# Two graph attention layers: the neighbour score as a column of the value matmuls, and row maxima turned in 32x32 blocks

## The chip, the cores and the metric

The kernel runs on one core of a Trainium2 chip. The metric is the device time of one execution in microseconds (us); lower is better. The engines are named as in the profile: PE (TensorE matmul), PEld (its weight load), DVE (VectorE), ACT (ScalarE), POOL (GpSimd), SP (SyncE, which issues most DMAs).

## The reference

The input is x (16 batches x 1024 nodes x 64 features, float32) and one adjacency matrix of 1024 x 1024. Four layers follow each other; each takes h = relu(layernorm(x)) and adds its result to x.

```python
def gat(h, W, a, adj):                     # layer 0 with elu, layer 3 with relu
    Wh = h @ W
    s1, s2 = Wh @ a[:64], Wh @ a[64:]
    e = leaky_relu(s1[:, :, None] + s2[:, None, :], 0.2) + mask
    return act(softmax(e, axis=2) @ Wh)
# layer 1: feat = softplus(c * x + b0); per feature softmax over neighbours of feat * wa + ba, times feat
# layer 2: four heads, h = x @ Wh.T; softmax(mask(h @ h.T)) @ h + bh; leaky_relu; one more such
#          layer over the heads' outputs with Wo; leaky_relu; layernorm with gamma, beta
```

## The kernel before, in words

**Data.** Each batch of x lies in SBUF as 128 partitions x 8 tiles (T = 8) of 64 features. One unit of work of the attention layers is one batch (layers 0 and 3) or one head of one batch (layer 2: 4 heads and one out unit a batch, 80 units). A unit has 8 steps jt, one for each 128 neighbours: a weight tile of 128 x 1024 is made in one of 8 `ring` buffers, and 32 matmuls (`weigh`, L1712) multiply it into the accumulators ACC with the values V. The column 0 of V's 65 columns carries a factor of the node, so that the sums of the weights come out beside the sums of the values.

**A unit of layers 0 and 3.** PE transposes the normalised batch (`turn_norm`, L1692), ACT writes its relu to `h_t` (L890). From `h_t` PE makes three things: the 64 value columns (`gat_columns`, L1753), the own scores f1 spread over all partitions in S (`gat_gain`, L1769), and the neighbour scores f2, 8 columns of one (`gat_peak`, L1734). Values and f2 go to the two AX banks, which a table (`AX_AT`, filled by the `place_` functions) hands out in program order. DVE copies f2 and takes its maximum over a partition (`node_max`, L1346 and L1348). PE spreads the 128 maxima over all partitions: `spread` (L1702) uses the column of maxima as weights, repeated, and the identity as the moving operand, so that each partition gets the 128 values in a row. DVE reduces them to the peak (`node_peak`, L1358), POOL makes two biases of it (L669, L671). ACT copies the values to V (L952), makes the exponentials of f2 with these biases (L958 to V's column 0, L960 to `pair_q`) and of the scores in S (L967, L970). POOL scales V by column 0 (L663). DVE makes the weight tiles, ring = max(S, pair_q) * mask (L1336). At the unit's end ACT copies ACC to `accs` (L895), DVE takes a reciprocal (L1370), and POOL divides (L639). In layer 0 POOL and ACT then make the elu (L643 above zero; L937 and L939 below) and POOL adds both parts to X (L649, L652); POOL also normalises the batches to come (L581 to L588).

**Order.** Each engine runs a program of its own, written out by hand, and waits on semaphores; an engine never passes a waiting instruction. While PE works at the sums of unit `cur`, it makes the next units' inputs at fixed steps (`gat_unit`):

```python
for jt in range(T):
    gat_sums(layer, cur, jt)
    if jt == 0 and cur + 1 < B:
        gat_nodes(layer, cur + 1)        # values, then f1
    if jt == 2 and cur + 2 < B:
        gat_peak(layer, cur + 2)         # f2
    if jt == T - 1 and cur + 2 < B:
        spread_peak(layer, cur + 2)
    if jt == T - 1 and cur + 3 < B:
        turn_norm(layer, cur + 3)
```

ACT's program of layer 0 for one `cur` is: `gat_sums` (accs), `h_relu` of cur + 2, statistics of a later batch, `gat_factors` of cur + 1 (copy of V, exponentials, scores), the elu of cur - 1, more statistics. V has three buffers, of which a unit of layers 0 and 3 uses two in turn.

**The dot layer (layer 2)** makes its weights by an exponential on ACT (L1092) and a mask on DVE (L1484); PE makes the products (L1895) and the sums (L1914). Each unit needs an upper bound of its scores: DVE sums squares (`norms`, L1513), takes their maximum over a partition (L1515), PE spreads it (L1702, the same `spread`), DVE reduces 128 columns (`bias`, L1521). The last out unit of the layer, LAST, is interleaved with the first units of layer 3 (`last_layer`); BEFORE is the unit ahead of it.

Of the kernel before, what the change touches and what calls it, by code (L numbers as in the profile page):

```python
# [11 lines left out]
P = 128  # L12
D = 64
# [17 lines left out]
def gnn_stack(nc, x, adj, w_gat0, w_gat0_t, a_gat0, w0, b0, wa, ba, wh_t, bh, wo_t, bo, gamma, beta,  # L31
# [9 lines left out]
    EARLY = 4  # L41

    with ExitStack() as ctx:
# [51 lines left out]
        V = sb("V", [P, 3, T, D + 2])  # L95
# [5 lines left out]
        f2 = sb("f2", [P, 2, T])  # L101
# [25 lines left out]
        norm2 = sb("norm2", [P, T])  # L127
# [34 lines left out]

        def chans(ap):

            return ap.unsqueeze(1).broadcast_to([P, T, D])
# [8 lines left out]

        def halves_of(ap):
            return ap.rearrange("p (h t) d -> p h t d", h=2)
# [4 lines left out]
            (w_gat[0:D, 0, 0:D], w_gat0), (w_gat[D:P, 0, 0:D], w_gat0),  # L181
            (w_gat[0:D, 1, 0:D], w_gat3), (w_gat[D:P, 1, 0:D], w_gat3),
# [49 lines left out]
        f2_copied = sem("f2_copied")  # L232
        f2_maxed = sem("f2_maxed")
# [93 lines left out]
        def gat_buf(layer, b):  # L327

            return 2 * ((b + layer // 3) % 2)
# [50 lines left out]
        def place_peak(layer, b):  # L380

            place_f2(layer, b)
            place_bias(layer, b)

# [4 lines left out]
        def place_f2(layer, b):  # L389

            for half in range(2):
                place(("GF", layer, b, half), half)

        def place_nodes(layer, b):

            for half in range(2):
                place(("GV", layer, b, half), half)

        def place_first_layer():

            place_norm(0, 0)
            place_peak(0, 0)
            place_nodes(0, 0)
            place_norm(0, 1)
            place_peak(0, 1)
# [4 lines left out]
        def place_beside(layer, cur):  # L410

            if cur + 1 < B:
                place_nodes(layer, cur + 1)
            if cur + 2 < B:
                place_peak(layer, cur + 2)
# [22 lines left out]
        for u in UNITS[:-1]:  # L438
# [11 lines left out]
            if u is BEFORE:  # L450
                place_norm(3, 0)
                place_peak(3, 0)
# [3 lines left out]
        place_nodes(3, 0)  # L456
        place_peak(3, 1)
        place_norm(3, 2)
        place_nodes(3, 1)
        place_f2(3, 2)  # L460
# [3 lines left out]
        place_nodes(3, FIRST)  # L464
        place_values(LAST)
        place_bound(LAST)
        place_peak(3, FIRST + 1)
        place_norm(3, FIRST + 2)
        for cur in range(FIRST, B):
            if cur > FIRST:  # L470
                place_beside(3, cur)
            else:
                place_nodes(3, cur + 1)
                place_peak(3, cur + 2)
                place_norm(3, cur + 3)
# [11 lines left out]
        AHEAD = 5  # L487

# [50 lines left out]
        def _(pool):  # L539
# [94 lines left out]
            def gat_divide(layer, b):  # L634
# [5 lines left out]
                if layer == 0:  # L640
# [4 lines left out]
            def gat_add(layer, b):  # L645

                if layer == 0:
# [230 lines left out]
        def _(act):  # L878
# [54 lines left out]
            def gat_below(b):  # L933

                act.wait_ge(gat_o, b + 1)
                wait(act, x_done[0], b)
                act.activation(below[:, :], o[:, :], ACT.Relu, scale=-1.0).then_inc(elu_below, 1)  # L937
                act.wait_ge(elu_below, b + 1)
                act.activation(below[:, :], below[:, :], ACT.Exp, scale=-1.0).then_inc(elu_exp, 1)  # L939

            def gat_factors(layer, b):

                gat_columns(layer, b)
                gat_gain(layer, b)

            def gat_columns(layer, b):

                n, par, buf = G0[layer] + b, b % 2, gat_buf(layer, b)
                for half in range(2):
                    k, at = AX_AT["GV", layer, b, half]  # L950
                    act.wait_ge(ax_full[k], at + 1)
                act.activation(halves_of(V[:, buf, :, 1:D + 1]), V_FULL, ACT.Copy).then_inc(gat_v_copied, 1)  # L952
                act.wait_ge(gat_v_copied, n + 1)
                for k in range(2):
                    act.sem_inc(ax_free[k], 1)
                act.wait_ge(f2_copied, n + 1)
                act.wait_ge(f2_biased, 2 * n + 2)
                act.activation(V[:, buf, :, 0], f2[:, par, :], ACT.Exp, bias=node_bias[:, par:par + 1], scale=SLOPE)\  # L958
                    .then_inc(node_made, 1)
                act.activation(pair_q[:, par, :], f2[:, par, :], ACT.Exp, bias=pair_bias[:, par:par + 1],  # L960
# [25 lines left out]
            def gat_layer(layer):  # L986
# [3 lines left out]
                for t in range(2, 5):  # L990
                    mask_copy(t)
                gat_columns(0, 0)
# [1055 lines left out]
```

## Time and profile before

| | |
|---|---|
| three runs | 1892.89, 1895.61, 1895.60 us; median 1895.60 |
| profiled execution, its own time | 1894.35 us |
| span of that execution in the trace | 1892.1 us |
| mean granted PE clock in it | 0.994 of full speed |
| busy: PE, PEld | 97%, 81% of the span |
| busy: DVE, ACT, POOL | 88%, 68%, 48% of the span |
| chain that ended last, by engine | PE 84%, POOL 8%, DVE 4%, issue 2%, ACT 1% |

The times are of whole executions; the trace is of one of them, and its span is a little shorter than that execution's time. The stages in the trace: layer 0 from about 12 to 225 us, the channel layer on PE to 405, the dot layer to 1680, layer 3 to 1890. A busy share is a mean over stages with different limits. The chain that ended last follows the work back from the end, at each step to what released it.

### The profile page before, as it was taken

To read this page: it belongs to the slowest core of one execution; us is meant where nothing else is said; L and a number is where in the kernel's file an instruction comes from. 1 tells how busy PE (TensorE), PEld (TensorE's weight loads), DVE (VectorE), ACT (ScalarE), POOL (GpSimd) and SP (SyncE) were. 2 spreads that over 40 slices of the span, in tenths; PEclk is the share of its full clock that TensorE was granted. 3 is DMA by queue.
4 is the path that set the end of the run, shared out by engine and by line. 5 is a ranking of instruction groups with operands and counts; after the bars stand their busy time and mean duration, and the time that the engine had idled before them with its cause. 6 is when DMAs were issued, how large, how long until landed. Compare 5 with 4: busy or idle time off the path is not lost.

```text
span 1892.1 us, 92007 instructions
## 1 busy us (share of the span) xinstructions
PE 1840.0 (97%) x42280; PEld 1531.0 (81%) x42280; DVE 1660.6 (88%) x1932; ACT 1285.1 (68%) x2052; POOL 907.5 (48%) x686
## 2 busy tenths in 40 slices
PE   7999899999999999999999999999999999999998
PEld 6887799987878788787888878878787878877887
DVE  6989899768898889988899888989988899888998
ACT  4998676446777777777777777777777777754332
POOL 6888999633233343424344342443334334264753
PEclk8999999999999999999999999999999999999999
DMA  7000000012111112221111211111111112201111
GB/s 192 4 4 4 3 2 3 2 25 36 37 36 36 36 36 37 34 38 31 36 34 35 38 34 36 36 36 36 36 37 36 36 35 32 42 3 26 26 32 31
DMA packets 134321, 61.02 MB, mean 32 GB/s; under 512 B 122416, under 2 KB 122672, under 8 KB 133936
## 3 DMA queue, kind: packets, MB, share of 16 engines
q1 hardware_dynamic: 131712, 54.55, 14.3%
q8 instruction: 332, 5.44, 1.2%
q10 hardware_dynamic: 2224, 0.59, 0.1%
q14 instruction: 53, 0.43, 0.1%
HBM read 8.98 MB, written 4.19 MB: 7 GB/s over the span
## 4 chain that ended last, share of the span: by engine, by line
PE 84%; POOL 8%; DVE 4%; issue 2%; ACT 1%; DMA 0%; ACTq 0%; POOLq 0%; DVEq 0%
PE ACC L1914 30%; PE S L1895 29%; PE S L1872 8%; PE ACC L1712 7%; PE AX L1957 3%; PE AX L1930 2%; DVE ring L1336 1%; PE AX L1702 1%; PE AX L1692 1%; POOL above L643 1%; PE S L1769 1%; POOL o L639 1%; DVE ring L1484 1%; PE AX L1753 1%; POOL X L649 1%
## 5 line engine op out<-in xcount | busy, mean ns | idle before, releaser
L1484 DVE TENSOR_TENSOR ring<-ring,mask_self_t 128x1024 f32<-128x1024 f32 x640 | 878.0, 1385 | 68.8 <-ACT ring L1092 61.1
L1092 ACT ACTIVATE ring<-S,dot_bias 128x1024 f32<-128x1024 f32 x640 | 711.5, 1113 | 274.3 <-PE S L1895 235.7
L1914 PEld LDWEIGHTS ACC<-V,ring 128*64 128x64 f32 x20480 | 706.7, 138 | 109.8 <-issue 13.2
L1914 PE MATMUL ACC<-V,ring 128*64 128x65 f32 x20480 | 708.0, 222 | 0.0
L1895 PE MATMUL S<-FA 128*64 128x512 f16 x5120 | 665.5, 380 | 1.1 <-ACT ring L1092 0.9
L1895 PEld LDWEIGHTS S<-FA 128*64 128x64 f16 x5120 | 268.6, 110 | 141.8 <-issue 10.9
L1336 DVE SCALAR_TENSOR_TENSOR ring<-S,pair_q,mask_t 128x1024 f32<-128x1024 f32 x256 | 313.9, 1273 | 16.5 <-issue 4.3
L1712 PEld LDWEIGHTS ACC<-V,ring 128*64 128x64 f32 x8192 | 253.3, 139 | 56.2 <-DVE ring L1336 34.7
L1712 PE MATMUL ACC<-V,ring 128*64 128x65 f32 x8192 | 270.4, 225 | 20.3 <-DVE ring L1336 11.5
L819 POOL TENSOR_TENSOR EV_both<-score,recip 128x512 f32<-128x512 f32 x64 | 96.8, 1512 | 263.9 <-DVE score L1494 263.8
L1872 PE MATMUL S<-parts,mask_t 128*128 128x128 bf16 x3072 | 173.8, 220 | 4.7 <-DVE o L1461 3.5
L1872 PEld LDWEIGHTS S<-parts,mask_t 128*128 128x128 bf16 x3072 | 173.2, 98 | 5.3 <-issue 5.3
L812 POOL TENSOR_TENSOR V<-v_plain,bh_bc 128x512 f32<-128x512 f32 x64 | 99.8, 1559 | 124.3 <-ACT v_plain L1119 124.3
L1502 DVE TENSOR_TENSOR HL<-v_plain,HL 128x512 f16<-128x512 f32 x80 | 77.0, 962 | 76.7 <-ACT HL L1124 76.7
L895 ACT ACTIVATE accs<-ACC 128x520 f32<-128x520 f32 x32 | 19.1, 597 | 90.7 <-PE ACC L1712 90.7
L819 POOL TENSOR_TENSOR relu_z<-score,recip 128x512 f32<-128x512 f32 x16 | 16.7, 1042 | 124.6 <-DVE score L1494 124.6
L557 POOL TENSOR_TENSOR st_x<-X,st_mean 128x512 f32<-128x512 f32 x20 | 33.5, 1676 | 75.0 <-DVE st_mean L1303 75.0
L600 POOL TENSOR_TENSOR ln_xc<-X,ln_mean 128x512 f32<-128x512 f32 x16 | 22.5, 1409 | 95.7 <-DVE ln_mean L1319 95.7
L802 POOL TENSOR_TENSOR sp_log<-relu_z,on_mean 128x512 f32<-128x512 f32 x16 | 30.5, 1906 | 74.5 <-DVE on_mean L1531 74.5
L663 POOL TENSOR_TENSOR V<-V 128x512 f32<-128x512 f32 x32 | 33.3, 1041 | 59.9 <-ACT V L958 59.8
L1459 DVE RECIPROCAL ch_rden<-S 128x512 f32<-128x512 f32 x15 | 50.3, 3351 | 10.6 <-PE S L1872 7.8
L1513 DVE TENSOR_REDUCE norm<-sq 128x8 f32<-128x512 f32 x80 | 54.0, 675 | 0.0
(149 smaller groups left out, 2076.6 us busy)
## 6 DMA issues: line engine op xcount, KB each, us to landing
FA<-FA SPq DMA_DIRECT2D x160, 128.0 KB, 2.3
X<-in_x SPq DMA_DIRECT2D x16, 256.0 KB, 4.8
ring<-in_adj SPq DMA_DIRECT2D x8, 512.0 KB, 8.1
out_x<-X SPq DMA_DIRECT2D x16, 256.0 KB, 2.6
FA<-HL SPq DMA_TRANSPOSE x80, 3.1
wh<-in_wh_t ACTq DMA_DIRECT2D x2, 64.0 KB, 6.5
bh_bc<-in_bh ACTq DMA_DIRECT2D x1, 128.0 KB, 9.9
w_gat<-in_w_gat ACTq DMA_DIRECT2D x4, 16.0 KB, 3.9
```

Source lines behind the costliest of these rows:

```text
L812: pool.tensor_tensor(V[:, u["n"] % 3, :, 1:D + 1], plain_of(u), chans(bias), ALU.add)\
L819: pool.tensor_tensor(dst, tiles(leaky[:, :]), cols(recip[:, :]), ALU.mult).then_inc(z_epi, 1)
L1092: act.activation(ring[:, jt, :], S[jt % 2][:, :], ACT.Exp, bias=dot_bias[:, n % 2:n % 2 + 1])\
L1336: dve.scalar_tensor_tensor(out=ring[:, jt, :], in0=S[par][:, :], scalar=pair_q[:, par, jt:jt + 1], in1=mask_t[:, jt, :], op0=ALU.max, op1= ...
L1484: dve.tensor_tensor(ring[:, jt, :], ring[:, jt, :], mask_self_t[:, jt, :], ALU.mult)\
L1502: dve.tensor_tensor(HL[:, par, :, D:2 * D], plain_of(u), HL[:, par, :, 0:D], ALU.subtract)\
L1513: dve.tensor_reduce(norm2[:, :], tiles(sq[:, :]), AX_X, ALU.add).then_inc(bound_dve, 1)
L1712: last = pe.matmul(acc_of(t)[rows, :], ring[:, jt, t * P + c * CUT:t * P + (c + 1) * CUT], values, start=(jt == 0 and t % 4 == 0), stop=(j ...
L1872: last = pe.matmul(S[par][:, t * P:(t + 1) * P], mask_t[:, j, t * P:(t + 1) * P], parts[:, k % 3, part, j, :], start=(j == 0 and part == 0 ...
L1895: last = pe.matmul(S[jt % 2][rows, cut], FA[:, buf, 0, jt * P + c * CUT:jt * P + (c + 1) * CUT], FA[:, buf, i, cut], start=(i == 0), stop= ...
L1914: last = pe.matmul(acc_of(t)[rows, :], ring[:, jt, t * P + c * CUT:t * P + (c + 1) * CUT], V[:, n % 3, jt, 1:D + 2], start=(jt == 0 and t ...
L1957: last = pe.matmul(AX[half][c * CUT:(c + 1) * CUT, t * width:(t + 1) * width], rows, w, start=(i == 0), stop=(i == chunks[-1]), skip_group ...
```

## The change

The f2 column moves into the value matmuls: `w_gat` now holds it as column 0 ahead of the 64 value columns, and `gat_columns` makes 65 columns for each tile. `gat_peak` on PE and its places in AX_AT are gone. The value matmuls of unit cur + 2 stand after the third tile of unit cur, where f2's stood. ACT copies all 65 columns to V one unit sooner; for that V has four buffers, and a unit uses three in turn. In layer 0 this copy (of cur + 2) stands ahead of the exponentials of cur + 1, in layer 3 behind them. DVE reads f2 from V's column 0.

The maxima of f2 and of the norms are reduced further before the spread: DVE transposes 32x32 blocks, so that the values of 32 partitions come to lie in one row, and reduces over 32; `spread` then moves 32 columns in place of 128, with a strided identity, and DVE's reductions behind it read 32.

For the last two batches of layer 0 (`ELU_SWITCH`) the elu is made in another way: POOL takes min(o, 0), ACT its exponential, DVE max(exp - 1, o), and POOL adds once. The start of layer 3 is put in an order that fits the earlier values.

On ACT, in the middle of layer 0, a unit stood so before (accs is the copy of the sums, h_t the relu, st_x the statistics, V<-AX the copy of the values, V<-f2 and pair_q the exponentials):

```order
L895 ACTIVATE accs<-ACC 128x520 [waits gat_o,pv_done]
L890 ACTIVATE h_t<-AX 128x512 [waits ax_full1]
L915 ACTIVATE st_x,st_shift<-X 128x64 [waits h_ready,late_squared,x_in12]
L915 ACTIVATE st_x,st_shift<-X 128x64 x7
L952 ACTIVATE V<-AX 128x8x64 [waits ax_full1,ax_full0]
L958 ACTIVATE V<-f2,node_bias 128x8 [waits gat_v_copied,f2_biased,f2_copied]
L960 ACTIVATE pair_q<-f2,pair_bias 128x8
L967 ACTIVATE S1<-S1,f2_peak 128x1024 [waits f1_full]
L970 ACTIVATE S1<-S1,pair_lift 128x1024 [waits gain_clamped]
```

and now:

```order
L895 ACTIVATE accs<-ACC 128x520 [waits gat_o,pv_done]
L890 ACTIVATE h_t<-AX 128x512 [waits ax_full1]
L915 ACTIVATE st_x,st_shift<-X 128x64 [waits h_ready,late_squared,x_in12]
L915 ACTIVATE st_x,st_shift<-X 128x64 x7
L949 ACTIVATE V<-AX 128x8x65 [waits ax_full1,ax_full0]
L964 ACTIVATE V<-f2,node_bias 128x8 [waits gat_v_copied,f2_biased,f2_copied]
L966 ACTIVATE pair_q<-f2,pair_bias 128x8
L973 ACTIVATE S1<-S1,f2_peak 128x1024 [waits f1_full]
L976 ACTIVATE S1<-S1,pair_lift 128x1024 [waits gain_clamped]
```

The rows stand in the same places, but the copy V<-AX is now that of unit cur + 2, where it was that of cur + 1; the exponentials behind it are still those of cur + 1.

On PE, the beginning of a unit of layer 0 before (ACC<-V,ring are the sums, AX<-w_gat,h_t 64x64 the values, 64x1 f2, S1<-h_t,w_gat the scores f1):

```order
L1712 MATMUL ACC<-V,ring 64x65 [waits weight_done,acc_copied,v_scaled]
L1712 MATMUL ACC<-V,ring 64x65 x15
L1753 MATMUL AX<-w_gat,h_t 64x64 [waits ax_free1,ax_free0]
L1753 MATMUL AX<-w_gat,h_t 64x64 x15
L1769 MATMUL S1<-h_t,w_gat 64x512 [waits weight_done]
L1769 MATMUL S1<-h_t,w_gat 64x512 x3
L1712 MATMUL ACC<-V,ring 64x65 [waits weight_done]
L1712 MATMUL ACC<-V,ring 64x65 x15
L1712 MATMUL ACC<-V,ring 64x65 [waits weight_done]
L1712 MATMUL ACC<-V,ring 64x65 x15
L1734 MATMUL AX<-w_gat,h_t 64x1 [waits ax_free1,ax_free0,h_ready]
```

and now:

```order
L1744 MATMUL ACC<-V,ring 64x65 [waits weight_done,acc_copied,v_scaled]
L1744 MATMUL ACC<-V,ring 64x65 x15
L1782 MATMUL S1<-h_t,w_gat 64x512 [waits weight_done]
L1782 MATMUL S1<-h_t,w_gat 64x512 x3
L1744 MATMUL ACC<-V,ring 64x65 [waits weight_done]
L1744 MATMUL ACC<-V,ring 64x65 x15
L1744 MATMUL ACC<-V,ring 64x65 [waits weight_done]
L1744 MATMUL ACC<-V,ring 64x65 x15
L1766 MATMUL AX<-w_gat,h_t 64x65 [waits ax_free1,ax_free0,h_ready]
L1766 MATMUL AX<-w_gat,h_t 64x65 x15
L1744 MATMUL ACC<-V,ring 64x65 [waits weight_done]
```

The value matmuls moved from behind the first tile to behind the third, took f2's place, and belong to a unit further ahead.

On DVE, in the dot layer, the bound of a unit before (ring<-ring,mask_self_t is the masking of a weight tile):

```order
L1513 TENSOR_REDUCE norm2<-sq 128x8 [waits sq_made]
L1515 TENSOR_REDUCE norm2_max<-norm2 128x1 [waits bound_dve]
L1484 TENSOR_TENSOR ring<-ring,mask_self_t 128x1024 [waits exp_done] x3
L1521 TENSOR_REDUCE norm2_all<-AX 128x1 [waits ax_full0]
L1523 TENSOR_SCALAR dot_bias<-norm2_all 128x1 [waits ax_free0]
```

and now:

```order
L1543 TENSOR_REDUCE norm2<-sq 128x8 [waits sq_made]
L1545 STREAM_TRANSPOSE norm2_turned<-norm2 128x32 [waits bound_dve]
L1547 TENSOR_REDUCE norm2_max<-norm2_turned 128x1 [waits bound_dve]
L1514 TENSOR_TENSOR ring<-ring,mask_self_t 128x1024 [waits exp_done] x3
L1553 TENSOR_REDUCE norm2_all<-AX 128x1 [waits ax_full0]
L1555 TENSOR_SCALAR dot_bias<-norm2_all 128x1 [waits ax_free0]
```

One transposition stands between the two reductions; the third reduction reads 32 columns of AX.

The diff, cut to its core:

```diff
-        V = sb("V", [P, 3, T, D + 2])
+        V = sb("V", [P, 4, T, D + 2])
...
+        def turned_cols(ap):
+            return ap.rearrange("p (g r) -> p g r", r=SQ)[:, :, 0:T]
...
-            return 2 * ((b + layer // 3) % 2)
+            return (0, 1, 2)[b % 3] if layer == 0 else (2, 3, 0)[b % 3]
...
# POOL
+                if layer == 0 and b >= ELU_SWITCH:
+                    pool.tensor_scalar(below[:, :], o[:, :], 0.0, None, ALU.min).then_inc(elu_below, 1)
...
# ACT
             def gat_columns(layer, b):
...
-                act.activation(halves_of(V[:, buf, :, 1:D + 1]), V_FULL, ACT.Copy).then_inc(gat_v_copied, 1)
+                act.activation(halves_of(V[:, buf, :, 0:D + 1]), V_GAT, ACT.Copy).then_inc(gat_v_copied, 1)
...
+            def gat_factors(layer, b):
+                gat_exponents(layer, b)
+                gat_gain(layer, b)
...
                     if late_stats(layer, cur) is not None:
                         late_shifts(late_stats(layer, cur))
+                    if cur + 2 < B:
+                        gat_columns(layer, cur + 2)
                     if cur + 1 < B:
                         gat_factors(layer, cur + 1)
...
                     if cur + 1 < B:
                         gat_factors(3, cur + 1)
+                    if cur + 2 < B:
+                        gat_columns(3, cur + 2)
...
# DVE
             def node_max(layer, b):
...
+                dve.wait_ge(gat_v_copied, n + 1)
                 wait(dve, pair_made, n - 1)
+                dve.tensor_copy(f2[:, par, 0:T], V[:, gat_buf(layer, b), :, 0]).then_inc(f2_copied, 1)
+                dve.wait_ge(f2_copied, n + 1)
+                dve.transpose(f2_turned[:, :], f2[:, par, :]).then_inc(f2_across, 1)
+                dve.wait_ge(f2_across, n + 1)
+                dve.tensor_reduce(f2_max[:, :], f2_turned[:, :], AX_X, ALU.max).then_inc(f2_maxed, 1)
...
+            def gat_elu(b):
+                dve.wait_ge(elu_exp, b + 1)
+                dve.scalar_tensor_tensor(out=o[:, :], in0=below[:, :], scalar=-1.0, in1=o[:, :],
+                                         op0=ALU.add, op1=ALU.max).then_inc(elu_made, 1)
...
             def norms(u):
...
-                dve.tensor_reduce(norm2_max[:, :], norm2[:, :], AX_X, ALU.max).then_inc(bound_dve, 1)
+                dve.transpose(norm2_turned[:, :], norm2[:, :]).then_inc(bound_dve, 1)
+                dve.wait_ge(bound_dve, n + 2)
+                dve.tensor_reduce(norm2_max[:, :], norm2_turned[:, :], AX_X, ALU.max).then_inc(bound_dve, 1)
...
# PE
             def spread(k, column):
                 for c in range(2):
-                    last = pe.matmul(AX[k][c * CUT:(c + 1) * CUT, 0:P], column.broadcast_to([P, CUT]), ident[:, :],
-                                     start=True, stop=True, skip_group_check=True)
+                    last = pe.matmul(AX[k][c * CUT:(c + 1) * CUT, 0:T * P // SQ], column.broadcast_to([P, CUT]),
+                                     turned_cols(ident[:, :]), start=True, stop=True, skip_group_check=True)
...
                     gat_sums(layer, cur, jt)
                     if jt == 0 and cur + 1 < B:
-                        gat_nodes(layer, cur + 1)
+                        gat_gain(layer, cur + 1)
                     if jt == 2 and cur + 2 < B:
-                        gat_peak(layer, cur + 2)
+                        gat_columns(layer, cur + 2)
```

## Rows read from the trace of the kernel before

**Rows 1.** Windows: busy us (x instructions) of each engine, granted clock, DMA share, GB/s.
```profile
85.90:155.00 69.10, 65.66 (x2020) 57.10 (x2016) 61.95 (x73) 63.05 (x265) 60.93 (x67) 1.00 0.02 4
...
440.00:1660.00 1220.00, 1218.20 (x26716) 977.01 (x26714) 1086.01 (x1289) 896.43 (x1128) 447.48 (x265) 1.00 0.18 36
```

**Rows 2.** Timeline, a unit of layer 0: start, duration, engine, line, operation, [idle before].
```profile
114.14 1.15 PE L1712 MATMUL ACC<-V,ring 128*64 128x65 f32 x32 [0.16 <-issue]
...
115.22 0.69 PE L1753 MATMUL AX<-w_gat,h_t 64*64 64x64 f32 x32
...
115.74 1.04 PE L1769 MATMUL S<-h_t,w_gat 64*64 64x512 f32 x8
...
116.72 0.58 ACT L952 ACTIVATE V<-AX 128x512 f32<-128x512 f32 x1
...
117.99 0.31 ACT L958 ACTIVATE V<-f,node_bias 128x8 f32<-128x8 f32 x1 [0.69 <-POOL pair_bias L671]
...
118.44 1.04 POOL L663 TENSOR_TENSOR V<-V 128x512 f32<-128x512 f32 x1 [0.55 <-ACT V L958]
...
118.72 0.64 PE L1734 MATMUL AX<-w_gat,h_t 64*64 64x1 f32 x32
...
119.30 4.89 PE L1712 MATMUL ACC<-V,ring 128*64 128x65 f32 x160
...
123.72 1.04 POOL L588 TENSOR_TENSOR ln_y<-ln_xc,st_rstd 128x512 f32<-128x512 f32 x1
...
125.63 1.15 PE L1712 MATMUL ACC<-V,ring 128*64 128x65 f32 x32 [0.16 <-issue]
```

**Rows 3.** Timeline, a unit of layer 3, the values and what follows on ACT.
```profile
1801.93 0.69 PE L1753 MATMUL AX<-w_gat,h_t 64*64 64x64 f32 x32
...
1802.78 0.60 ACT L952 ACTIVATE V<-AX 128x512 f32<-128x512 f32 x1 [1.24 <-PE AX L1753]
...
1803.62 0.31 ACT L958 ACTIVATE V<-f,node_bias 128x8 f32<-128x8 f32 x1 [0.24 <-ACT V L952]
```

**Rows 4.** Timelines of PE and POOL, first to last units of layer 0.
```profile
45.79 0.69 PE L1753 MATMUL AX<-w_gat,h_t 64*64 64x64 f32 x32
...
161.46 0.69 PE L1753 MATMUL AX<-w_gat,h_t 64*64 64x64 f32 x32
...
164.22 1.04 POOL L663 TENSOR_TENSOR V<-V 128x512 f32<-128x512 f32 x1 [1.52 <-ACT V L958]
...
186.80 0.69 PE L1753 MATMUL AX<-w_gat,h_t 64*64 64x64 f32 x32
...
190.02 1.04 POOL L663 TENSOR_TENSOR V<-V 128x512 f32<-128x512 f32 x1 [2.37 <-ACT V L958]
```

**Rows 5.** Window and PE timelines at the end of layer 0.
```profile
217.70:221.10 3.40, 2.67 (x50) 2.67 (x52) 3.40 (x4) 1.32 (x3) 3.32 (x3) 0.50 0.02 5
...
218.43 4.23 PE L1712 MATMUL ACC<-V,ring 128*64 128x65 f32 x96 [2.80 <-DVE ring L1336]
...
250.61 5.58 PE L1872 MATMUL S<-parts,mask_t 128*128 128x128 bf16 x68 [3.50 <-DVE o L1461]
```

**Rows 6.** Chain that ended last (one piece), then timelines, dot layer.
```profile
1671.21 0.22 PE AX L1702 x4
...
479.94 0.44 PE L1702 MATMUL AX<-ident,norm_max 128*64 128x128 f32 x4
...
1656.59 0.16 DVE L1515 TENSOR_REDUCE norm_max<-norm 128x1 f32<-128x8 f32 x1
...
1656.81 0.44 PE L1702 MATMUL AX<-ident,norm_max 128*64 128x128 f32 x4
```

**Rows 7.** Timelines, start of layer 3 (DVE, PE) and a steady unit (DVE).
```profile
1683.74 1.28 DVE L1336 SCALAR_TENSOR_TENSOR ring<-S,pair_q,mask_t 128x1024 f32<-128x1024 f32 x1 [4.29 <-issue]
...
1701.92 2.08 PE L1957 MATMUL AX<-wo,z_t 128*64 128x64 f32 x64 [1.05 <-ACTq L955]
...
1811.26 0.29 DVE L1358 TENSOR_REDUCE f_peak<-AX 128x1 f32<-128x128 f32 x1 [0.28 <-PE AX L1702]
```

More of the change, by code:

```diff
@@ L463, in gnn_stack @@
         place_norm(3, 3)
-        place_nodes(3, FIRST)
         place_values(LAST)
         place_bound(LAST)
[L467 to L475, printed above, removed]
+        for cur in range(FIRST - 1, B):
+            place_beside(3, cur)
         def stats_before(layer):
@@ L645, in gat_add @@
             def gat_add(layer, b):
-                if layer == 0:
+                if layer == 0 and b >= ELU_SWITCH:
+                    pool.wait_ge(elu_made, b + 1)
+                    pool.tensor_tensor(x_of(b), x_of(b), tiles(o[:, :]), ALU.add).then_inc(x_done[layer], 1)
+                elif layer == 0:
                     pool.wait_ge(elu_above, b + 1)
@@ L933, in gat_below @@
             def gat_below(b):
-                act.wait_ge(gat_o, b + 1)
-                wait(act, x_done[0], b)
-                act.activation(below[:, :], o[:, :], ACT.Relu, scale=-1.0).then_inc(elu_below, 1)
+                if b < ELU_SWITCH:
+                    act.wait_ge(gat_o, b + 1)
+                    wait(act, x_done[0], b)
+                    act.activation(below[:, :], o[:, :], ACT.Relu, scale=-1.0).then_inc(elu_below, 1)
                 act.wait_ge(elu_below, b + 1)
[L939 to L944, printed above, removed]
+                act.activation(below[:, :], below[:, :], ACT.Exp, scale=-1.0 if b < ELU_SWITCH else 1.0)\
+                    .then_inc(elu_exp, 1)
             def gat_columns(layer, b):
-                n, par, buf = G0[layer] + b, b % 2, gat_buf(layer, b)
+                n, buf = G0[layer] + b, gat_buf(layer, b)
                 for half in range(2):
@@ L989, in gat_layer @@
                 h_relu(0, 0)
-                for t in range(2, 5):
-                    mask_copy(t)
+                mask_copy(2)
                 gat_columns(0, 0)
+                mask_copy(3)
+                mask_copy(4)
+                gat_exponents(0, 0)
                 mask_copy(5)
@@ L1416, in gat_layer @@
                                 channel_part(k, k % 2, (1, 3, 6, 7).index(jt))
+                        if jt == 7 and cur > ELU_SWITCH:
+                            gat_elu(cur - 1)
             def channel_step(k, par):
@@ L1723, in gat_sums, with gat_columns @@
                 weigh(tile_of(layer, b, jt), jt, V[:, buf, jt, 0:D + 1])
[L1725 removed]
+            def gat_columns(layer, b):
                 w = layer // 3
                 pe.wait_ge(h_ready, H0[layer] + b + 1)
[L1729 to L1747 removed]
                 for half in range(2):
```

146 lines of the change are left out of this document (66 added, 80 removed).

## The prediction

> **What bounds the kernel now.** I looked first at the busy table by stage [rows 1]. In the long dot layer (440 to 1660 us) PE is busy 1218.20 of 1220.00 us, so there only PE time counts, or a wait that PE gains. In the middle of layer 0 (85.9 to 155.0) no engine is full: PE 65.66, ACT 63.05, POOL 60.93 and DVE 61.95 of 69.10. Such a stage is bounded by a loop that passes through several engines, and a busy share says nothing of what an edit costs. So I laid one unit of it out as a timeline [rows 2]. A unit starts with PE's first weight tile, at s = 114.14; the next starts at 125.63, so the period is 11.49 us. Within it ACT waits 0.69 us for POOL's pair_bias, makes the exponentials at 117.99, and POOL in turn waits 0.55 us for them before it scales V at 118.44. POOL then works without a long pause until ln_y (123.72, 1.04 us long), PE transposes that, and the next unit begins. The loop is POOL, ACT, POOL; from the exponentials to the next first tile it takes 125.63 - 117.99 = 7.64 us. The copy of V sits just ahead of them on ACT at 116.72, with no wait before it, because PE made the values early, at 115.22.
>
> **Layer 0, the loop.** The change makes the values one unit sooner, but after the third tile of the unit instead of the first, where the f2 matmuls stood. On ACT the copy of these values is put ahead of the exponentials of the next unit. ACT runs in order, so the exponentials, which needed only POOL's bias, now wait for PE's third tile.
>
> On PE, f2 started at s + 4.58 (118.72 - 114.14). The values no longer lie ahead of it, which moves everything up by 0.52 (115.22 to 115.74), so the new value matmuls start at s + 4.06.
>
> From their start to ACT's copy, and from that to the exponentials: in layer 3 [rows 3] ACT already waits for the values. There the matmuls start at 1801.93, the copy at 1802.78 (0.85 later), the exponentials at 1803.62 (0.84 later). So in layer 0 the copy would start at s + 4.91, the exponentials at s + 5.75; before it was 117.99 - 114.14 = 3.85.
>
> The rest of the loop is unchanged, 7.64. The period becomes 5.75 + 7.64 = 13.39 us, **+1.9 us a unit**.
>
> The first unit of this form has its values at 45.79 and the eleventh at 161.46 [rows 4]: ten periods, 115.67 us, of which 134.0 would be made, +18.3. Three more units follow, longer ones, where POOL's scaling already came later: 164.22 - 161.46 = 2.76 and 190.02 - 186.80 = 3.22 after the values' start. With the new order it is 4.06 - 1.08 (first tile to values, 115.22 - 114.14) + 0.85 + 0.84 + 0.45 (117.99 to 118.44) = 5.12 by the same mark, so +2.4 and +1.9; at their mean three units give +6.4. Together **+24.7**. The lower end is one in which the three long units absorb it (+18).
>
> PE's removed f2 matmuls (32 in 0.58 us, 118.72 to 119.30) are worth nothing here, and neither does the 65th column of the values cost anything: the loop runs past PE with room. No DMA is added or moved, the two more small copies of w_gat's columns come once, at the start, for which I take 0, with 1 us either way. The work of DVE (a copy, a transpose, a reduction per unit) lies beside the loop too. node_max now waits for ACT's copy, which would end at s + 5.5, and the sixth weight tile stands behind it on DVE; PE wants that tile at about s + 4.64 + 3 x 0.98 = s + 7.6, so there is little room, but what is late there comes out of PE's pause at the unit's end. If that cover were gone it would cost 0.2 us a unit, one small DVE operation.
>
> **Layer 0, the clock.** PE's own work of a unit does not grow, so the idle time does. The last sums would end at s + 4.06 + 0.58 (values) + 4.75 (160 matmuls in 4.89 less a pipeline tail, from 119.30) = s + 9.4, and ln_y is ready for PE at s + 5.75 + 6.77 (117.99 to 123.72 + 1.04) = s + 12.5: about 3.1 us idle in each unit. In the trace an idle time of 2.80 us ahead of 218.43 is followed by a granted clock of 0.50 (1.2 instead of 2.4 GHz) from 217.7 to 221.1 [rows 5], and 96 sums then took 4.23 us, where 96 at the rate of 119.30 take 2.93. So one fall costs 1.3 us at most and about 1.2 in the loop, where a piece of it is in the shadow of the idle time. It lies between the first tile and the values, that is on the loop. I take 8 of 13 units, **+10**; bounds 0 (none falls) and +16 (all).
>
> **Layer 0, the end.** For the last two batches one POOL pass, and the ACT pass ahead of the exponential, are dropped. PE waits 3.50 us ahead of 250.61 for what follows from it [rows 5]; that bounds the gain. I take **-2.3**, two thirds, ends 0 and -3.5.
>
> **Dot layer.** The transposition of the bound costs DVE one more operation in each of the 80 units, and the spread on PE reads 32 instead of 128 columns. A spread costs 0.22 us in the chain (1671.21) [rows 6]. Its new price lies between 32 matmuls of one column in 0.58 (118.72 to 119.30), that is 0.07 for four, and 65 columns, 160 in 4.89, that is 0.12 for four [rows 2]. I take 0.09, which saves 0.13. But norm_max begins at 1656.59 and lasts 0.16, and PE's spread begins at 1656.81 [rows 6]: at that place PE hangs on it, and it is so in 30 of the 80 units, from the one with its spread at 479.94 to this one, by my count of the gap; in one the slack is 0.23 and in 49 at least 0.39 us. The trace of before has no such transposition; the nearest rows are small DVE operations, 0.16 (norm_max) and 0.29 (f_peak over 128 columns, [rows 7]). I take 0.18, with two handovers 0.24. In 30 units 0.24 - 0.13 = 0.11 is lost (+3.3), in 50 units 0.13 is won (-6.5): **-3.2**. If the transposition is hidden everywhere, -10.4; if the spread saves nothing, 30 x 0.24 = +7.2.
>
> A rule of the Trainium skill speaks against this part. The page "TensorE: Matmul & The Clock Gate", section "LDWEIGHTS (loading the stationary operand)", says a weight load takes its columns divided by 1.2, in ns; the spread still loads 64 columns, four times, so by my estimate 0.21 us would remain and nothing be saved. The rows here speak against that: 160 sums, each with a load of 64 columns, took 30.6 ns apiece [rows 2].
>
> **Layer 3.** Here the new copy stands behind the exponentials, so nothing waits for it. A steady unit gains where PE and DVE hand over to each other, at the spread and the peak: DVE's reduction waits 0.28 for PE at 1811.26 [rows 7]. With 32 columns that is 0.13 for the spread and 0.10 for the reduction, against 0.03 for one more step in the chain of node_max: -0.2 a unit, eleven units, -2.2. The start of the layer is put in another order. DVE was idle 4.29 us ahead of 1683.74, and PE waited 1.05 ahead of 1701.92 for ACT's copy, which is now behind it; I take -3.1 of these 5.3 together (0 to -5). **-5.3**, from -2 to -7.
>
> **The sum.** 24.7 + 10 - 2.3 - 3.2 - 5.3 = +23.9. The profiled execution took 1894.35 us, so 1918.3; the median of the three runs, 1895.60, lies 1.25 above it, so on that scale 1919.5. I say **1919.0**.
>
> **The rivals.**
>
> **First**, the clock holds. The loop lengthens, but the spread of f2_max, now free to run in the pause, splits the idle time. Then 1894.35 + 13.9 = 1908.3. For it: the 3.1 is only 0.3 over the shortest idle time with a fall. 22%.
>
> **Second**, the wait does not bind, and the kernel is **faster**. The mechanism: PE reaches its third tile early relative to ACT. It decides at copy's start: ACT comes free for it at s + 2.58 (116.72), and if it could start by s + 3.01 (3.85 less 0.84), the exponentials would stay where they are. That needs PE 1.9 us further ahead of ACT than in [rows 2]. Then only the other terms are left: -2.3 - 3.2 - 5.3, 1883.6. Against it: PE's first tile itself hangs on ln_y, at the end of the same loop, so it cannot run ahead. 8%.
>
> **Third**, the spread is bound by its weight loads and saves nothing. +7.2 instead of -3.2 in the dot layer, and with the forecast otherwise, 1929. It is also what the rule on weight loads would make of it. 8%.
>
> **Fourth**, the change does little: the loop lengthens by only a part, because something in it (POOL's other work, ACT's statistics) is moved into the new wait, and the gains cancel it, 1891 to 1900. 5%.
>
> The forecast itself, loop and clock, has 57%; within it the number of falls spreads it from 1909 to 1926.
>
> **How the numbers follow.** About 0.2%, 3.8 us, is what a measurement of this kernel can tell from no change. Faster: the second rival alone, 0.08. Same: the last, 0.05. Slower: the rest, 0.87. The range 1901 to 1932 takes in the forecast with all its bounds, the held clock and the load-bound spread, and leaves out the faster case and part of the last.
>
> **What would show it.** In the changed profile a layer 0 unit should last 13.4 to 14.6 us; ACT's copy of V should wait over 2 us for PE's value matmuls, POOL's scaling over 2 us for ACT's exponentials; PE's granted clock in the middle of layer 0 should lie below 1.00 with 3 us idle ahead of the transposes of ln_y. In the dot layer the spread should take about 0.1 us, with DVE's norm_max 0.2 us later. Layer 3 should be some 5 us shorter. I am wrong if the period of layer 0 stays at 11.5, or if DVE's transposition takes far more than 0.3 us.

## The result, and the profile after

The change took 1947.84 us (median of 4 runs, 1943.47 to 1950.80) against 1895.61 of before: a ratio of 1.0276, 95% interval 1.0262 to 1.0290. It is slower, as forecast, but by 52 us and not by 24; 1919.0 (1901 to 1932) was too low. The profiled execution took 1943.47 us, span 1941.4, 49.3 more than before; the median lies 4.4 us above it, where before it was 1.25.

To see where the time went I cut both traces at the same places: the first score matmul (S<-h_t,w_gat) of the third, the 13th and the 16th unit of layer 0, the first spread of the dot layer, a late one, and the end. The times between them, us:

| stretch | before | change | difference | forecast |
|---|---|---|---|---|
| start to the third unit | 46.31 | 48.05 | +1.7 | 0 |
| ten units of layer 0 | 115.66 | 147.56 | +31.9 | +18.3, and falls |
| the three long units | 37.15 | 49.10 | +12.0 | +6.4, and falls |
| end of layer 0 and channel layer | 200.40 | 196.34 | -4.1 | -2.3 |
| dot layer, first to late spread | 1257.28 | 1259.28 | +2.0 | -3.2 |
| end of the dot layer and layer 3 | 235.32 | 241.10 | +5.8 | -5.3 |

The falls of the clock were forecast at +10 for the second and third line together. The first line differs by up to 5 us between runs of these kernels, so nothing is read from it.

The windows of the change (busy us of PE, PEld, DVE, ACT, POOL, then granted clock, DMA share, GB/s):

```profile
105.00:145.00 40.00, 31.73 (x912) 27.36 (x912) 31.29 (x39) 31.58 (x131) 30.33 (x33) 1.00 0.01 3
145.20:152.40 7.20, 6.16 (x70) 4.10 (x72) 4.92 (x5) 4.34 (x26) 5.16 (x7) 0.53 0.01 2
...
85.90:155.00 69.10, 55.01 (x1468) 46.61 (x1466) 51.27 (x62) 51.83 (x218) 50.02 (x55) 0.93 0.01 3
440.00:1660.00 1220.00, 1209.56 (x26565) 965.10 (x26564) 1095.91 (x1360) 888.82 (x1119) 447.31 (x263) 1.00 0.19 36
```

The third and fourth answer to [rows 1]. In the same 69.1 us of layer 0 every engine now does less, none is nearer to full. PE has pauses at the full clock (31.73 of 40.00 busy) and at half of it (6.16 of 7.20): each engine waits for another. One unit at the full clock, from the timeline (start, duration, engine, line, operation, [idle before]), answers to [rows 2]:

```profile
120.14 1.15 PE L1744 MATMUL ACC<-V,ring 128*64 128x65 f32 x32 [0.15 <-issue]
...
124.26 0.69 PE L1766 MATMUL AX<-w_gat,h_t 64*64 64x65 f32 x32
...
125.11 0.60 ACT L949 ACTIVATE V<-AX 128x520 f32<-128x520 f32 x1 [2.29 <-PE AX L1766]
...
125.95 0.31 ACT L964 ACTIVATE V<-f,node_bias 128x8 f32<-128x8 f32 x1 [0.24 <-DVE f L1367]
...
126.41 1.04 POOL L663 TENSOR_TENSOR V<-V 128x512 f32<-128x512 f32 x1 [2.51 <-ACT V L964]
...
131.69 1.04 POOL L581 TENSOR_TENSOR ln_y<-ln_xc,st_rstd 128x512 f32<-128x512 f32 x1
...
132.78 0.66 PE L1724 MATMUL AX<-ident,ln_y 128*128 128x128 f32 x4 [2.72 <-POOL ln_y L581]
...
133.59 1.15 PE L1744 MATMUL ACC<-V,ring 128*64 128x65 f32 x32 [0.15 <-issue]
```

This is the forecast loop nearly to the digit: the value matmuls start at s + 4.12 (forecast 4.06), ACT's copy waits 2.29 us for them and starts at s + 4.97 (4.91), the exponentials at s + 5.81 (5.75), POOL waits 2.51 for them, and the unit lasts 133.59 - 120.14 = 13.45 us (13.39). PE's pause ahead of ln_y is 2.72 (3.1), and 2.68 to 2.73 in all twelve such units; the clock falls behind nine of these pauses and not behind those of 105.87, 119.33 and 132.78.

What the forecast did not have stands in layer 3, in the timeline of a steady unit of the change:

```profile
1875.84 1.27 POOL L655 TENSOR_TENSOR X<-X,o 128x512 f32<-128x512 f32 x1
1875.94 1.20 DVE L1367 COPY f<-V 128x8 f32<-128x8 f32 x1
...
1877.17 0.21 DVE L1369 STREAM_TRANSPOSE f_turned<-f 128x32 f32<-128x32 f32 x1
1877.42 0.18 DVE L1371 TENSOR_REDUCE f_max<-f_turned 128x1 f32<-128x32 f32 x1
...
1878.85 2.35 PE L1744 MATMUL ACC<-V,ring 128*64 128x65 f32 x64 [0.91 <-DVE ring L1359]
```

DVE's copy of 128x8 values lasts 1.20 us and ends with POOL's addition to X; the next weight tiles stand behind it, and PE waits 0.91 for them. Before the change the copy read PSUM (AX) and was short, also beside a TENSOR_TENSOR of POOL:

```profile
1806.08 1.04 POOL L581 TENSOR_TENSOR ln_xc<-X,st_mean 128x512 f32<-128x512 f32 x1
...
1806.84 0.15 DVE L1346 COPY f<-AX 128x8 f32<-128x8 f32 x1
...
1812.83 0.69 PE L1753 MATMUL AX<-w_gat,h_t 64*64 64x64 f32 x32
```

A unit takes 11.70 us, where before it was 10.90 (1801.93 to 1812.83 for the value matmuls).

### The profile page after: what moved, and what is told of

It is laid out like the page before. It is cut to its first block, busy times and chain, and to the rows that moved or that the text cites. A ratio compares the mean times of both kernels' runs of the same rounds, so it can differ in the third digit from the quotient of the medians.

```text
span 1941.4 us, 89972 instructions
## 1 busy us (share of the span) xinstructions
PE 1841.1 (95%) x41256; PEld 1522.0 (78%) x41256; DVE 1694.0 (87%) x2050; ACT 1284.9 (66%) x2050; POOL 905.7 (47%) x684
## 4 chain that ended last, share of the span: by engine, by line
PE 61%; DVE 21%; POOL 6%; ACT 5%; issue 5%; DMA 0%; ACTq 0%; POOLq 0%; DVEq 0%
PE S L1906 20%; PE ACC L1925 19%; DVE ring L1514 10%; PE S L1883 8%; PE ACC L1744 6%; DVE ring L1359 4%; PE AX L1968 3%; ACT ring L1103 3%; PE AX L1941 2%; DVE norm L1543 1%; DVE HL L1532 1%; PE S L1782 1%; PE AX L1724 1%; POOL above L640 1%; POOL o L632 1%
## 5 line engine op out<-in xcount | busy, mean ns | idle before, releaser
L1514 DVE TENSOR_TENSOR ring<-ring,mask_self_t 128x1024 f32<-128x1024 f32 x640 | 864.4, 1370 | 59.8 <-ACT ring L1103 54.6
L1925 PEld LDWEIGHTS ACC<-V,ring 128*64 128x64 f32 x20480 | 707.2, 138 | 109.7 <-issue 13.2
L1925 PE MATMUL ACC<-V,ring 128*64 128x65 f32 x20480 | 708.3, 222 | 0.1
L1906 PEld LDWEIGHTS S<-FA 128*64 128x64 f16 x5120 | 263.2, 110 | 141.4 <-issue 10.9
L1744 PEld LDWEIGHTS ACC<-V,ring 128*64 128x64 f32 x8192 | 266.0, 144 | 79.8 <-DVE ring L1359 43.9
L1744 PE MATMUL ACC<-V,ring 128*64 128x65 f32 x8192 | 286.1, 230 | 33.9 <-DVE ring L1359 22.2
L812 POOL TENSOR_TENSOR V<-v_plain,bh_bc 128x512 f32<-128x512 f32 x64 | 113.6, 1774 | 119.0 <-ACT v_plain L1130 119.0
L1532 DVE TENSOR_TENSOR HL<-v_plain,HL 128x512 f16<-128x512 f32 x80 | 91.5, 1143 | 72.9 <-ACT HL L1135 72.9
L1724 PE MATMUL AX<-ident,ln_y 128*128 128x128 f32 x192 | 35.4, 313 | 33.6 <-POOL ln_y L581 32.7
L949 ACT ACTIVATE V<-AX 128x520 f32<-128x520 f32 x32 | 19.3, 604 | 61.8 <-PE AX L1766 61.8
```

The source lines that it names most:

```text
L812: pool.tensor_tensor(V[:, u["n"] % 3, :, 1:D + 1], plain_of(u), chans(bias), ALU.add)\
L1514: dve.tensor_tensor(ring[:, jt, :], ring[:, jt, :], mask_self_t[:, jt, :], ALU.mult)\
L1532: dve.tensor_tensor(HL[:, par, :, D:2 * D], plain_of(u), HL[:, par, :, 0:D], ALU.subtract)\
L1724: last = pe.transpose(AX[k][:, q * P:(q + 1) * P], ln_y[:, q * P:(q + 1) * P], ident[:, :])
L1744: last = pe.matmul(acc_of(t)[rows, :], ring[:, jt, t * P + c * CUT:t * P + (c + 1) * CUT], values, start=(jt == 0 and t % 4 == 0), stop=(j ...
L1906: last = pe.matmul(S[jt % 2][rows, cut], FA[:, buf, 0, jt * P + c * CUT:jt * P + (c + 1) * CUT], FA[:, buf, i, cut], start=(i == 0), stop= ...
```

## The experiments

Each is compared with before on its own chip. "Ten units" and so on are the stretches of the table.

**1. The exponentials ahead of the copy.** ACT's order in layer 0:

```diff
+                    if cur + 1 < B:
+                        gat_exponents(layer, cur + 1)
                     if cur + 2 < B:
                         gat_columns(layer, cur + 2)
                     if cur + 1 < B:
-                        gat_factors(layer, cur + 1)
+                        gat_gain(layer, cur + 1)
```

> In layer 0 ACT makes the two exponentials of unit cur + 1 ahead of the copy of unit cur + 2, instead of behind it; all else is the change. Theory A (the exponentials queue behind a copy that waits for PE's third tile): a unit of layer 0 returns from 13.46 us to about 11.5, PE's pauses of 2.73 us and the falls of its clock with them go, layer 0 shortens by some 40 to 45 us, total 1901 to 1909. Rival B (the longer chain on DVE, copy, transposition and reduction behind ACT's copy, bounds the unit by itself): the period stays above 12.5 and the total above 1920.

Measured: 1926.39 us, 1.0170 (1.0155 to 1.0185). Ten units took 137.36 us, so still 13.7 each: rival B's numbers, and my theory wrong in the form that I gave it. But DVE is not the reason. The timeline, in a unit with its first part at half the clock:

```profile
114.70 0.59 ACT L895 ACTIVATE accs<-ACC 128x520 f32<-128x520 f32 x1
...
115.38 2.00 PE L1746 MATMUL ACC<-V,ring 128*64 128x65 f32 x32 [2.48 <-issue]
...
117.87 0.29 ACT L964 ACTIVATE V<-f,node_bias 128x8 f32<-128x8 f32 x1
...
121.70 0.60 ACT L949 ACTIVATE V<-AX 128x520 f32<-128x520 f32 x1 [3.35 <-PE AX L1768]
```

The exponentials come early again (117.87, s + 2.5), and POOL is served. But ACT now waits 3.35 us at the copy with all the rest of its unit behind it: the scores, the elu, the statistics, and last the copy of the sums to accs, without which PE may not begin the next unit. That copy ends at 115.29, and PE, idle for 2.48 us, starts at 115.38. So there were two loops through the same wait; freeing the one leaves the other.

**2. PE kept busy in its pause.** Forty matmuls of the identity, whose result nothing reads, are added ahead of the transposes of ln_y in 13 units:

```diff
                     if jt == T - 1 and cur + 3 < B:
+                        if layer == 0:
+                            k = take_bank(AX_AT["T", layer, cur + 3])
+                            for _ in range(40):
+                                pe.matmul(AX[k][:, 0:P], ident_bf[:, :], ident_bf[:, :], start=True, stop=True,
+                                          skip_group_check=True)
                         turn_norm(layer, cur + 3)
```

> The change, with 40 matmuls of the identity (no result used, into a free bank of AX) in PE's pause at the end of the first 13 units of layer 0, ahead of the transposes of ln_y. Theory A (the lengthened loop alone costs about 26 us in layer 0, and the rest of its 45.5 us are falls of the clock, each dearer than the 1.2 us I took): no granted clock of 0.50 between 60 and 240 us, the period 13.46 in each of the units 1 to 10, total about 18 to 20 us shorter than the change, 1927 to 1930. Rival B (a fall costs the 1.2 us of the prediction, ten falls 12 us, and the rest is a longer wait in the loop): total 1934 to 1938. Rival C (the clock falls whether PE is busy in the pause or not): no change, 1944 to 1950.

Measured: 1929.07 us, 1.0185 (1.0170 to 1.0200), 18.8 below the change: theory A. The windows:

```profile
62.00:210.00 148.00, 140.87 (x3771) 124.06 (x3772) 119.58 (x152) 112.66 (x452) 107.08 (x116) 1.00 0.01 4
228.00:235.20 7.20, 6.47 (x98) 4.64 (x96) 6.64 (x9) 5.50 (x11) 6.74 (x8) 0.53 0.01 2
```

The clock stays at 1.00 from 62 to 210 us. Two falls follow, at 214.6 and 228.3 us: they lie in the last units, after the added matmuls, but still inside the 240 us that theory A had named. Ten units take 135.24 us: 134.0 was forecast for the loop. Against the change's 147.56 that is 12.3 us for the seven falls in this stretch, 1.8 each.

**3. f2 taken by a reduction.** One instruction:

```diff
-                dve.tensor_copy(f2[:, par, 0:T], V[:, gat_buf(layer, b), :, 0]).then_inc(f2_copied, 1)
+                dve.tensor_reduce(f2[:, par, 0:T], V[:, gat_buf(layer, b), :, 0:1], AX_X, ALU.max).then_inc(f2_copied, 1)
```

> The change, with DVE's copy of f2 out of V (128x8, 1.20 us in a steady unit of layer 3, 0.17 in layer 0) written as a reduction over one element, which does the same work. Theory A (the copy, SBUF to SBUF, waits for POOL's addition to X, which runs just then and ends with it; a reduction doesn't): the operation takes about 0.16 us in layer 3, its units return from 11.70 to 10.7 to 10.9 us, 9 to 11 us less in total, 1936 to 1940. Rival B (the copy is slow for its strided source or waits for ACT's write of V): as slow as before, 1944 to 1950. Rival C (the operation gets short, but another wait in layer 3 takes its place): period above 11.3, under 4 us less.

Measured: 1934.96 us (1930.83 to 1939.15), 1.0214 (1.0194 to 1.0234). The runs scatter with the falls in layer 0, so the reading rests on the stretch of layer 3: 230.31 us against 241.10, and a steady unit 10.73. About 0.6 of these 10.8 us is not the copy but a fall of the clock at 1749.7 us in the change's profile, which this one hasn't (the same fall makes layer 3 of experiment 8 below 0.55 longer than that of 7). The timeline:

```profile
1876.80 1.28 POOL L655 TENSOR_TENSOR X<-X,o 128x512 f32<-128x512 f32 x1
1876.98 0.15 DVE L1367 TENSOR_REDUCE f<-V 128x8 f32<-128x8 f32 x1
```

The same values from the same place beside the same addition, in 0.15 us: theory A.

**4. The dot layer's bound as before.** No transposition in `norms`, 128 columns in `spread` and `bias` for the dot layer alone.

> The change, with the bound of the dot layer made as before (no transposition, the spread of 128 columns, the reduction of 128); the attention layers keep theirs. Theory A (DVE is full in two units of each batch, the transposition adds there what it lasts, +0.45 and +0.15 us, and three units win 0.13 each: +0.2 a batch): dot layer 2 to 4 us shorter, total 1943 to 1946. Rival B (the shorter spread wins more than the transposition costs, and the 2 us lie in the phase of POOL's work): dot layer 3 to 10 us longer, total 1951 or more.

Measured: 1943.42 us (1940.06 to 1949.26), 1.0253 (1.0236 to 1.0270). The total tells nothing, since the runs scatter by 9 us with the falls in layer 0 (ten units 152.99 in the profiled execution). The dot layer took 1259.07 us, where the change took 1259.28: 0.2 shorter, by itself neither theory. From the eleventh unit on, the turned bound does lose 0.2 us a batch (+0.45, +0.15 and three times -0.13), as theory A has it; but in the first batch the plain bound falls 2.5 us behind the turned one, once. The traces show why. PE's pause ahead of ln_y in this batch is 1.79 us with the plain bound and 0.91 with the turned one, which gives 0.85; and behind the longer pause the clock fell to 0.50 in this run and in experiment 6, the other one with the plain bound, but not in the kernel before (first two lines before the change, the others experiment 6):

```profile
447.79 0.66 PE L1692 MATMUL AX<-ident,ln_y 128*128 128x128 f32 x4 [1.79 <-POOL ln_y L615]
449.00:452.40 3.40, 3.40 (x82) 2.73 (x78) 1.45 (x3) 2.43 (x3) 0.00 (x0) 1.00 0.02 5
...
440.89 0.66 PE L1722 MATMUL AX<-ident,ln_y 128*128 128x128 f32 x4 [1.81 <-POOL ln_y L608]
442.10:445.50 3.40, 3.40 (x44) 2.55 (x40) 0.94 (x1) 1.60 (x2) 0.00 (x0) 0.50 0.02 5
```

From the fourth spread to the fifth it took 18.56 us in both runs with the fall and 16.93 before the change: the fall costs 1.6 us. Without it the plain bound would be 1.8 us shorter here than the change's, just under theory A's 2 to 4. The kernel before, with the plain bound and no fall, is 2.0 shorter.

**5. The copy late.** ACT's copy behind exponentials and scores in layer 0, node_max two tiles later:

```diff
-                    if cur + 2 < B:
-                        gat_columns(layer, cur + 2)
                     if cur + 1 < B:
                         gat_factors(layer, cur + 1)
+                    if cur + 2 < B:
+                        gat_columns(layer, cur + 2)
...
-                        if jt == 5 and cur + 2 < B:
+                        if jt == 7 and cur + 2 < B:
                             node_max(layer, cur + 2)
```

> The change, with ACT's copy of unit cur + 2 behind the exponentials and the scores of cur + 1 in layer 0 (as layer 3 has it), and DVE's node_max behind the eighth weight tile instead of the sixth. Theory A, as the run with the exponentials ahead of the copy left it (not the exponentials but everything that ACT still has to do in the unit stands behind the wait for PE's third tile, down to the copy of the sums, for which PE's next unit waits; a copy that finds its values ready costs nothing): a unit of layer 0 takes 11.4 to 11.7 us, no falls of the clock in units 1 to 10, total 1899 to 1908. Rival B (the third tile is too late for DVE's f2 chain wherever the copy stands): 12.5 us or more a unit, total above 1918.

Measured: 1896.98 us, 1.0007 (0.9998 to 1.0017): theory A, 2 us below its range. Ten units take 115.60 us, before the change it was 115.66. The timeline:

```profile
103.44 1.15 PE L1744 MATMUL ACC<-V,ring 128*64 128x65 f32 x32 [0.97 <-ACT accs L895]
...
107.55 0.70 PE L1766 MATMUL AX<-w_gat,h_t 64*64 64x65 f32 x32
...
108.97 0.60 ACT L949 ACTIVATE V<-AX 128x520 f32<-128x520 f32 x1
...
114.92 1.15 PE L1744 MATMUL ACC<-V,ring 128*64 128x65 f32 x32 [0.97 <-issue]
```

The values still start at s + 4.11, after the third tile. Only now ACT comes to the copy when they are done (no wait at 108.97), and the unit lasts 11.48 us. PE's pause is 0.97, and no fall follows in these ten units.

**6 to 8. What the rest is worth.** With the late copy of 5 and the reduction of 3: the bound of the dot layer as before (6), turned (7), and chosen by unit (8, plain for the second head and the out unit):

```diff
+    PLAIN = (0, 1)
...
+                if u["n"] % 5 in PLAIN:
+                    dve.tensor_reduce(norm2_max[:, :], norm2[:, 0:T], AX_X, ALU.max).then_inc(bound_dve, 2)
+                    return
                 dve.transpose(norm2_turned[:, :], norm2[:, :]).then_inc(bound_dve, 1)
```

> The run before, with f2 taken by a reduction and the bound of the dot layer made as before: what is left of the change are the 65-column values, the earlier start of layer 3, the turned peak of the attention layers and the elu of the last two batches. Theory A: layer 0 as before the change, its end 4 us shorter, the dot layer as before, layer 3 about 4 us shorter: 1885 to 1890. Rival B (the gains in layer 3 and at the end of layer 0 were only the echo of the long layer 0): 1892 to 1898.

> As the run before, but with the change's transposed bound in the dot layer: the difference of the two is the price of the transposition with nothing else changed and no falls of the clock. Theory A: 2.5 to 3.5 us longer than it, +0.45 and +0.15 in two units of a batch, -0.13 in three. Rival B (the price depended on what came before): under 1 us.

> As the run before, but the bound is made as before the change (128 columns, no transposition) for the second head and the out unit of a batch, where PE hangs on DVE's norm_max, and turned for the other three units. Theory A (the transposition costs only where DVE is full, and the short spread wins 0.13 where it isn't): 48 units win 0.13, some 6 us shorter than with the bound made as before, 1879 to 1884. Rival B (DVE is full over several units, and what a transposition adds in the units ahead is paid in the second head): 0 to 3 us shorter, 1883 to 1890.

| run | us | ratio to before, 95% | dot layer, us | layer 3, us |
|---|---|---|---|---|
| 6, plain | 1884.22 | 0.9944 (0.9927 to 0.9961) | 1259.10 | 230.27 |
| 7, turned | 1883.42 | 0.9937 (0.9922 to 0.9952) | 1259.36 | 230.30 |
| 8, by unit | 1881.89 | 0.9929 (0.9914 to 0.9944) | 1257.11 | 230.85 |

All three lie 0.6 to 0.7% below before, clear of the noise. 6 came out just below its range. 7 is only 0.3 us longer than 6 in the dot layer, and no longer in the total. But 6 has the fall of the clock shown under experiment 4, and 7 and 8 don't have it. Without the 1.6 us that it costs, the transposition's price is 1.9 us, between theory A (2.5 to 3.5) and rival B (under 1), and close to the 2.0 by which the change's dot layer is longer than before. In its units 8 gives rival B, though its total lies in theory A's range: of the turned units two win 0.13 us, but the second head, now plain, still loses 0.25 and the out unit 0.06, because DVE is full over several units and comes late from the ones ahead. A batch comes out even; of the 2.0 us that 8 gains on 6 in the dot layer, 1.6 is the fall that 8 hasn't, and the rest comes from the first batch. It is the best kernel here, 13 us below before.

**9. The elu as before**, on top of 7 (`ELU_SWITCH = B`, no `gat_elu`):

> As the run with the late copy and the reduction (transposed bound), but the elu of the last two batches of layer 0 is made as before. Theory A (the new elu is what shortened the stretch from layer 0's last scores to the first bound of the dot layer by 4 us): that stretch 3 to 4.5 us longer, total 1886 to 1888. Rival B (the stretch shortened for the earlier values, the elu is hidden): under 1 us longer, 1883 to 1884.5.

Measured: 1888.54 us, 0.9964 (0.9951 to 0.9977), 5.1 longer than 7; the stretch from the 16th unit to the first spread takes 199.09 against 195.97, and the three long units 0.6 more: theory A, though the total is 0.5 above its range. Part of it is again the clock: with the old elu PE waits 3.35 us ahead of 247.34 and the clock falls there, as it did before the change; in 7 this pause is 1.42 and no fall follows.

**10 and 11. The two parts of experiment 5 apart,** each alone on the change.

> The change with ACT's copy behind exponentials and scores in layer 0, but DVE's node_max where the change has it, ahead of the last weight tiles. Theory A (ACT's order is the main cause; node_max then waits for a copy that comes at s + 6.5 to 7.1, and the last two tiles stand behind it, which costs PE 0.5 to 1 us a unit): 12.0 to 12.5 us a unit, total 1903 to 1910. Rival B (PE's pause covers it): 11.5 us, total 1895 to 1899, as with both parts.

> The change with DVE's node_max behind the eighth weight tile in layer 0, ACT's order as in the change. Theory A (node_max was not what held the unit): period 13.4 and more with the falls of the clock, total 1940 to 1952. Rival B (DVE's wait for ACT's copy ahead of the last tiles was part of the loop): period 12.5 or less, under 1925.

Measured: with ACT's order alone 1897.05 us, 1.0014 (1.0004 to 1.0024), ten units 115.02: as good as both, rival B; DVE waits 0.68 us for the copy, but the tiles behind it hold PE for 0.31 only, ahead of a pause of 0.41. With node_max alone 1947.48 us, 1.0280 (1.0263 to 1.0296): the change again. So the order of three calls on ACT makes 1947.8 - 1897.1 = 50.8 us, nearly all of the result.

## Why the prediction was right and wrong

- **The loop of layer 0** was right in its place and its size, 13.45 us against 13.39 a unit, ten units 135.24 against 134.0 with the clock held (its own 13.39 makes 133.9). What it named as held up, the exponentials and POOL behind them, was only half: in experiment 1 they were freed and the unit took as long, since the copy of the sums stands behind the same wait. [rows 1] had it: ACT was busy 63.05 of 69.10, so a wait of 2.3 us on ACT, wherever it stands, cannot be made up before accs.
- **The clock**: right that it falls, wrong in size. "I take 8 of 13 units, +10" at 1.2 each; there were ten falls in layer 0 by windows of 0.4 us, half of them about 7 us long where the one of [rows 5] lasted 3.4, and seven cost 12.3 us. I took the price from a fall outside the loop; in the loop, as I read it, a slow first half of a unit delays the values and with them all that follows. The runs scatter over 7 us, where before they lay within 4.4.
- **The three long units**: "+6.4" without falls; with the clock held to 210 us (experiment 2) it was still +9.8 (46.98 against 37.15), two falls of the clock among them. The mean of two rows did not hold for units whose DVE and PE wait at other places; how much of it is clock I did not take apart.
- **Layer 3** is the step that failed most: "-5.3" was +5.8. I priced one more step in the chain of node_max at 0.03, a copy like the one before. But before, DVE copied f2 out of PSUM; now it reads V in SBUF while POOL adds to X. The prediction's "a copy, a transpose, a reduction per unit" counted operations and not where they read. The copy went from 0.15 us to 1.12 to 1.24 in nine units, and PE's next weight tiles stand behind it. Without that wait the stretch is 5.0 us shorter than before (230.31 against 235.32): the -5.3 was near the sum of all the rest.
- **The dot layer**: "-3.2" was +2.0 (1259.28 against 1257.28, no fall of the clock in either). The spread did get 0.13 us shorter in three units of five, as priced, but the two units that hang on DVE lost 0.45 and 0.15, not 0.11 each, because DVE's additions of the units ahead are still owed there (in experiment 8 the second head loses 0.25 with a plain spread). A batch loses 0.2 us in place of winning 0.17; the shorter pause of the first batch gives 0.85 back, once. One such unit of the change, in the timeline, answers to [rows 6]; PE waits where before it just didn't:

```profile
1085.54 0.21 DVE L1545 STREAM_TRANSPOSE norm_turned<-norm 128x32 f32<-128x32 f32 x1
1085.79 0.19 DVE L1547 TENSOR_REDUCE norm_max<-norm_turned 128x1 f32<-128x32 f32 x1
...
1086.03 0.31 PE L1734 MATMUL AX<-ident,norm_max 128*64 128x32 f32 x4 [0.47 <-DVE norm_max L1547]
...
1086.17 1.04 PE L1906 MATMUL S<-FA 128*64 128x512 f16 x8
```
- **The spread's price**: the rival that it stays bound by its weight loads is out. PE goes from the spread to the next matmul in 1086.17 - 1086.03 = 0.14 us, in the unit shown above. By the Trainium skill, "TensorE: Matmul & The Clock Gate", section "LDWEIGHTS (loading the stationary operand)", four loads of 64 columns would be an estimated 0.21; no run here shows that.
- **The end of layer 0**: -2.3 forecast, -4.1 measured; experiment 9 puts 3.1 of it at the elu, and 0.6 more in the long units.

The misses add up: layer 3 with 11.1, layer 0 with 43.9 - 34.7 = 9.2 us, the dot layer with 5.2, the start with 1.7 and the scatter of the runs (median against profiled execution, 3.1) with rounding 3.4, less 1.8 at the end of layer 0: the 28.8 that the forecast was short. No one of them alone explains why the time left the range: without layer 3's 11.1 it would be 1936.7, still above 1932.

## What to carry to other kernels

When an edit makes an in-order engine wait earlier in its unit, list everything that it does until the point where somebody waits for it, and not only the next instruction: here the cure was to put the copy behind work that was ready, with no other change. An input made one unit sooner buys nothing if its consumer is also moved up to it. And when an operand moves from PSUM to SBUF, look who else uses SBUF at that moment; a 128x8 copy can last as long as the neighbour's 128x512 addition.

## What the runs showed that I had not expected

**DVE's copy waits beside some of POOL's operations and not beside others.** In layer 3 the copy took 1.12 to 1.24 us in nine units and ended each time 0.03 us after POOL's addition to X. The Trainium skill, "SBUF — State Buffer", section "SBUF: two separate sides", says that DVE in a two-port mode, into which an fp32 copy from SBUF to SBUF goes, and POOL take a port pair by an exclusive lock; the trace agrees for POOL's addition to X, which began first each time. In experiment 10 the same copy falls beside POOL's TENSOR_SCALAR, which reads SBUF too:

```profile
118.02 1.93 POOL L640 TENSOR_SCALAR above<-o 128x512 f32<-128x512 f32 x1 [0.16 <-POOL o L632]
...
118.49 0.17 DVE L1367 COPY f<-V 128x8 f32<-128x8 f32 x1 [0.68 <-ACT V L949]
```

It takes 0.17 us there, in all eleven units of layer 0 where the two overlap (0.16 to 0.17). But in experiment 5 two of five copies beside the same operation, at 121.96 and 133.45 us, lasted 0.60 and 0.61 us and ended 0.03 after it. So the lock as the page has it, for any operation of POOL and its whole length, was not seen in the eleven, as far as POOL's spans can be trusted; for them the measurement decides. When this operation holds the copy up stays open.

**Equal pauses, unequal clock.** Pauses of PE of 2.68 to 2.73 us were followed by a fall to 0.50 in nine units and by none in three; the falls lasted some 3.5 or some 7 us. In the first batch of the dot layer a pause of 1.79 us was followed by none before the change and by a fall in experiment 4. How many units are hit changes from one execution to the next: the ten units took 147.56 us in the change and 152.99 in experiment 4, whose code is the same up to there. That fits the spread of the change's four runs, 1943.47 to 1950.80 us.
